# A post-norm decoder layer on one core: casts of the block sums moved from GpSimd to ScalarE, with reorders on VectorE and TensorE

## The chip, the core and the metric

The kernel runs on one NeuronCore of one Trainium2 chip. The core has five engines that run their own instruction queues side by side and meet only at semaphores: TensorE (PE: matrix products into the eight PSUM banks), VectorE (DVE), ScalarE (ACT), GpSimd (POOL) and SyncE (SP, which here only issues DMAs). An instruction that waits for a semaphore holds up everything behind it on its engine. The metric is the device time of one execution in microseconds (us), lower is better, as the median of several runs.

## What is computed

```python
x = _layernorm(x + self_attention(x))                # 8 sequences, 128 tokens, 512 features
x = _layernorm(x + cross_attention(x, ctx, mask))    # 32 heads of 128
x = _layernorm(x + feed_forward_with_experts(x))

# cross attention, where the change lies:
x = _rmsnorm(hidden_states, ln_weight)
h_q = (x @ w_q.T).reshape(b, lq, H, DH)
h_k = (key_value_states @ w_k.T).reshape(b, lk, H, DH)
h_v = (key_value_states @ w_v.T).reshape(b, lk, H, DH)
score = jnp.einsum('bqhd,bkhd->bhqk', h_q, h_k)
score = score + position_bias[None]
score = jnp.where(m, score, -jnp.inf)
score = jax.nn.softmax(score, axis=-1)
attn = jnp.einsum('bhqk,bkhd->bqhd', score, h_v).reshape(b, lq, H * DH)
out = attn @ w_out.T
```

All matrix products of weights are made in float32 from two parts: each operand is a high part (a cast to a shorter float, `_hi`) and a low part (the operand less its high part, `_lo`), and a product is hi*hi + hi*lo + lo*hi.

## The kernel before

`self_attention` is the first stage (to about 205 us), `layer` the rest. In `layer` the 32 heads go in 16 groups g of two heads, and each group is four tiles s = 0 to 3 (one head for half of the batch). Number the tiles n = 4g + s. Per tile PE makes the scores (L2060), the products ahead for a later tile, the transposes of the probabilities of tile n-1 (L2067), two v projections (L760), between them attention times v of tile n-1 (L2077, `pv`), and two output products (L2090). DVE adds mask and bias and takes the maximum (`masked_scores`, L1580 and `nmx` L1585), divides by the sum (`normalise`, L1589 to L1591), makes low parts (`at_lo` L1597, `lo` L1571, `lo_op` L1603) and adds the output to `acc` (L1634). ScalarE makes the exponentials (`exps`, L1331), the high parts and the copies out of PSUM (`prT` L1339, `v` L1324, `at_hi` L1345). POOL adds mask and bias into `bm` (`bias_mask`, L1045), which `masked_scores` needs.

Groups 0 and 1 are *plain*: the q and k projections are made directly, twelve products each (L760). Groups 2 to 15 (`SEVEN` = 2) take the projection of q and of k as a 2 x 2 block product by seven products p1 to p7 instead of eight (Strassen's scheme, L1936). `unit(w, ...)` makes one of them, w = 0 for q and w = 1 for k. That needs seven sums of x and context blocks, named S1k, S2k, S4k, S3k, S3q, S2q, S4q, and S1q, which stays in SBUF in the place of a quarter of `xnT`. POOL forms them during tiles 2 to 7: `combine` adds or subtracts 128 x 1024 numbers (L1052), `hi_of` casts (L1055), `block_lo` subtracts (L1058). SP's `keep` stores each as high and low part into `block_sums` in HBM (L970). From there POOL's `load_sums` brings one block after another into two ring slots of 1 MB (L1068) in each later group, behind a tiny *gate* instruction (L1067) that waits until the product that read the slot is over. The scratch areas are four quarters `area(0)` to `area(3)` of `stage`, and `U_` (= `mem.u`). `three_turns` (L1145 to L1153) and `last_turn` combine the weight blocks; ScalarE's `hi_op` and DVE's `lo_op` split them. `copy_p1` (L1366) copies product 1 from PSUM into the same `mem.u`.

There is no scheduler: each engine's order is written out in its block function. POOL's order in the stretch of the sums is

```python
            bias_mask(0, 2, True)
            k_differences()
            bias_mask(0, 3, True)
            k_first()
            k_fourth()
            k_second()
            bias_mask(1, 0, False)
```

and goes on with `k_fourth_split`, `k_third_split`, mask of tile 5, `q_third`, `q_second`, mask of tile 6, `q_third_split`, `q_fourth`, mask of tile 7, `q_first`, `q_second_split`, `q_fourth_split`, `q_first_split`, the first two ring loads and `three_turns(2)`.

## Time and profile before

| | us |
|---|---|
| median of 3 runs | 1101.55 (1100.03 to 1103.22) |
| the profiled execution | 1104.81 |
| its span, first to last instruction | 1103.0 |
| PE busy | 1036.4 |
| DVE busy | 764.7 |
| ScalarE busy | 501.2 |
| POOL busy | 482.1 |

The page gives for each engine its busy time; a group view gives the instructions of one line with their mean duration and the idle time of the engine ahead of them, with what ended it. A timeline gives single instructions with their start and duration. Durations on PE overlap, since products are pipelined: the distance between starts is what one costs. An idle time of an engine costs time only where that engine is the one that the end waits for.

### The profile page before, as it was taken

What the parts mean: (1) busy time and instruction counts of PE and PEld (TensorE: products, weight loads), DVE (VectorE), ACT (ScalarE), POOL (GpSimd) and SP (SyncE); (2) the same over time, 40 slices, a digit from 0 to 9 for tenths busy, and PEclk for the clock granted to TensorE, in tenths of its full rate; (3) what the DMA queues carried; (4) which work ended last, traced back from release to release, by engine and by line L of the source; (5) the groups of instructions that cost most, each with busy time, mean ns of one, the idle gap of its engine ahead of it and who ended that gap; (6) DMA issues with size and microseconds to landing.
All of it is one profiled execution on the core that took longest, in us unless ns stands there. A gap on an engine that the chain in (4) does not pass through costs nothing.

```text
span 1103.0 us, 20540 instructions
## 1 busy us (share of the span) xinstructions
PE 1036.4 (94%) x6354; PEld 898.0 (81%) x6354; DVE 764.7 (69%) x2269; ACT 501.2 (45%) x1377; POOL 482.1 (44%) x545
## 2 busy tenths in 40 slices
PE   7899989986999999999999999999999999999995
PEld 6677767876888888888888888888888888888884
DVE  5799989666667575757576666767675757576883
ACT  4889886441434343434343434444343434343421
POOL 7576665798734242423333242423242424242142
PEclk9999989998999999999999999999999999999998
DMA  4301002242355546372728374636455463636001
GB/s 149 125 18 52 2 1 68 76 157 117 131 211 184 206 141 227 120 247 100 255 95 287 95 252 140 240 139 227 155 198 192 155 212 135 247 100 232 28 20 58
DMA packets 44588, 159.77 MB, mean 145 GB/s; under 512 B 4736, under 2 KB 21504, under 8 KB 31616
## 3 DMA queue, kind: packets, MB, share of 16 engines
q0 software_dynamic: 14528, 105.91, 26.9%
q1 hardware_dynamic: 30016, 53.32, 14.8%
q8 instruction: 22, 0.36, 0.1%
q14 instruction: 22, 0.18, 0.1%
HBM read 149.78 MB, written 9.44 MB: 144 GB/s over the span
## 4 chain that ended last, share of the span: by engine, by line
PE 60%; issue 13%; DVE 11%; DMA 8%; POOL 5%; ACT 3%; POOLq 0%; SPq 0%; DVEq 0%; ACTq 0%
PE bank L1936 19%; PE bank L760 13%; PE bank L2090 12%; DMA ring<-block_sums 7%; PE bank L2077 4%; PE bank L2060 4%; PE bank L2108 3%; DVE sm L481 2%; PE bank L2067 2%; POOL bm L1045 2%; POOL pool_gate L1067 1%; POOL ring L1068 1%; DVE alpha L557 1%; DMA stage<-in_wq 1%; ACT pr L1331 1%
## 5 line engine op out<-in xcount | busy, mean ns | idle before, releaser
L1331 ACT ACTIVATE pr<-sm,nmx 128x128 f32<-128x128 f32 x256 | 99.8, 391 | 191.1 <-DVE nmx L1585 190.8
L1045 POOL TENSOR_TENSOR bm<-mask,bias 128x512 f32<-128x512 f32 x64 | 84.6, 1323 | 225.6 <-DVE nmx L1585 223.6
L1634 DVE TENSOR_TENSOR acc<-acc,bank 128x512 f32<-128x512 f32 x128 | 86.2, 684 | 81.7 <-PE bank L2090 81.7
L1067 POOL TENSOR_TENSOR pool_gate<-eps 128x1 f32<-128x1 f32 x96 | 45.5, 474 | 193.9 <-PE bank L1936 193.9
L1936 PE MATMUL bank<-ring,wqk_hi 128*128 128x512 f32 x392 | 110.9, 405 | 15.0 <-DMA ring<-block_sums 14.6
L1324 ACT COPY v<-bank 128x256 f32<-128x256 f32 x124 | 45.9, 370 | 126.8 <-PE bank L760 79.1
L2090 PE MATMUL bank<-wo_hi,at_hi 128*128 128x512 f32 x256 | 100.7, 393 | 0.3 <-DVE acc L1634 0.3
L2090 PE MATMUL bank<-wo_lo,at_hi 128*128 128x512 f32 x256 | 100.2, 391 | 0.0
L2090 PE MATMUL bank<-wo_hi,at_lo 128*128 128x512 f32 x256 | 100.0, 390 | 0.0
L1603 DVE TENSOR_TENSOR wqk_lo<-qk_raw,wqk_hi 128x512 fp32r<-128x512 f32 x98 | 92.6, 946 | 9.6 <-ACT wqk_hi L1360 9.6
L1936 PEld LDWEIGHTS bank<-ring,wqk_hi 128*128 128x128 f32 x392 | 67.8, 189 | 28.1 <-DMA ring<-block_sums 17.2
L760 PE MATMUL bank<-wv_hi,cT_hi 128*128 128x256 f32 x512 | 89.5, 297 | 0.3 <-DVE wv_lo L1891 0.3
L2077 PE MATMUL bank<-prT,v 128*128 128x128 f32 x512 | 69.9, 281 | 14.4 <-ACT prT L1339 14.4
L760 PE MATMUL bank<-wv_hi,cT_lo 128*128 128x256 f32 x512 | 82.6, 284 | 0.0
L760 PE MATMUL bank<-wv_lo,cT_hi 128*128 128x256 f32 x512 | 82.5, 284 | 0.0
L1339 ACT COPY prT<-bank 128x512 f32<-128x512 f32 x64 | 37.3, 582 | 96.2 <-PE bank L2067 96.2
L2077 PEld LDWEIGHTS bank<-prT,v 128*128 128x128 f32 x512 | 65.4, 196 | 16.9 <-ACT prT L1339 15.5
L1597 DVE TENSOR_TENSOR at_lo<-bank,at_hi 128x512 fp32r<-128x512 f32 x64 | 44.0, 687 | 48.0 <-ACT at_hi L1345 48.0
L760 PEld LDWEIGHTS bank<-wv_hi,cT_hi 128*128 128x128 f32 x512 | 73.1, 191 | 4.6 <-issue 0.5
L760 PEld LDWEIGHTS bank<-wv_hi,cT_lo 128*128 128x128 f32 x512 | 70.9, 192 | 0.0
L760 PEld LDWEIGHTS bank<-wv_lo,cT_hi 128*128 128x128 f32 x512 | 70.8, 192 | 0.0
L2060 PEld LDWEIGHTS bank<-kT,qT 128*128 128x128 f32 x512 | 66.7, 191 | 4.8
(289 smaller groups left out, 2633.0 us busy)
## 6 DMA issues: line engine op xcount, KB each, us to landing
ring<-block_sums POOLq DMA_DIRECT2D x98, 1024.0 KB, 5.6
qk_raw<-in_wqk SPq DMA_DIRECT2D x56, 256.0 KB, 5.8
o_raw<-in_wo SPq DMA_DIRECT2D x16, 512.0 KB, 3.3
v_raw<-in_wv SPq DMA_DIRECT2D x15, 512.0 KB, 8.8
block_sums<-stage SPq DMA_DIRECT2D x12, 512.0 KB, 3.6
acc<-in_x POOLq DMA_DIRECT2D x1, 2048.0 KB, 8.3
qk_raw<-in_wqk SPq DMA_DIRECT2D x4, 512.0 KB, 6.0
bias<-in_bias SPq DMA_DIRECT2D x16, 128.0 KB, 2.1
```

What stands on the lines that cost most here:

```text
L760: ins = nc.tensor.matmul(out, lhs, rhs, start=start and i == 0, stop=i == len(pairs) - 1)
L1045: nc.gpsimd.tensor_tensor(bm[:, s % 2], mask[:, HALF * (s // HG):HALF * (s // HG + 1), :], bias[:, i:i + 1, :].broadcast_to([P, HALF, T]), ...
L1067: nc.gpsimd.tensor_tensor(pool_gate[:, BLOCKS.index(name):BLOCKS.index(name) + 1], eps[:, 0:1], eps[:, 0:1], ALU.add)
L1324: nc.scalar.copy(v[:, b, :], PX[b % 2][:, 0:HG * DH2]).then_inc(s_vc, 1)
L1331: e = nc.scalar.activation(pr[:, s % 2, k], sm[:, s % 2, k], ACT.Exp, bias=nmx[:, s % 2, k:k + 1], accum_out=sums[:, s % 2, k:k + 1])
L1597: nc.vector.tensor_tensor(at[1][:, s // HG, i], PO[:], f32(at[0][:, s // HG, i]), ALU.subtract).then_inc(s_al, 1)
L1603: nc.vector.tensor_tensor(part_of(slot, 1), block_of(qk_raw, raw), f32(part_of(slot, 0)), ALU.subtract).then_inc(s_op, 1)
L1634: nc.vector.tensor_tensor(acc[:, b], acc[:, b], PX[b % 2][:], ALU.add).then_inc(s_acc, 1)
L1936: ins = nc.tensor.matmul((PQ, PK)[w][:], lhs, rhs, start=i == 0, stop=i == len(pairs) - 1)
L2060: ins = nc.tensor.matmul(S[s % 2][:, tok], qT[:, s % 2, tok], kT[:, s % 2, tok], start=True, stop=True)
L2077: ins = nc.tensor.matmul(PO[:, k * T:(k + 1) * T], v[:, half * HALF + k, i * DH2:(i + 1) * DH2], prT[:, k], start=True, stop=True)
L2090: ins = nc.tensor.matmul(PX[b % 2][:], at[p][:, half, i, tok], wo[q][:, i, :], start=k == 0 and (p, q) == PARTS[0], stop=k == HG - 1 and ( ...
```

## The change

- `combine` and `block_lo` on POOL work in two halves of 512 columns each, where they took 1024 in one instruction.
- The eight casts (`hi_of`) leave POOL. ScalarE makes them in `sums_hi`, at the ends of tiles: S1k at the end of tile 2, S2k and S4k of tile 3, S3k of tile 4, S3q of tile 5, S2q, S4q and S1q of tile 6. It waits there for POOL's sums (`s_made`, counted in halves) and, where it overwrites an area, until the block in it is stored. `block_lo` waits for the cast (`s_sums_h`). The semaphore `s_s1q` goes; `s_ready` counts its step too.
- DVE makes the masked scores ahead of `lo(wo, ...)` in the plain tiles with s = 2.
- DVE's `experts_constants` (13 small instructions) moves from the end of tile 3 to tile 60, in the last group.
- In the seven-product groups product 5 is made for k (w = 1) ahead of q (w = 0), and DVE adds them in that order.
- In `hi_op` the wait for the products of A11 is on q's counter instead of k's.

```diff
-                sp.wait_ge(s_ready, BLOCKS.index(name) + 1)
+                sp.wait_ge(s_ready, 2 * BLOCKS.index(name) + 2)
...
             def combine(out, in0, in1, op):
-                made.link(nc.gpsimd.tensor_tensor(out, in0, in1, op))
-
-            def hi_of(out, raw):
-                made.link(nc.gpsimd.tensor_copy(out, raw))
+                for c in range(2):
+                    made.link(nc.gpsimd.tensor_tensor(out[:, c], in0[:, c], in1[:, c], op))
 
             def block_lo(name, out, raw, hi):
-                nc.gpsimd.tensor_tensor(out, raw, f32(hi), ALU.subtract).then_inc(s_ready, 1)
-                pool.wait_ge(s_ready, BLOCKS.index(name) + 1)
+                pool.wait_ge(s_sums_h, BLOCKS.index(name) + 1)
+                for c in range(2):
+                    nc.gpsimd.tensor_tensor(out[:, c], raw[:, c], f32(hi[:, c]), ALU.subtract).then_inc(s_ready, 1)
+                    pool.wait_ge(s_ready, 2 * BLOCKS.index(name) + c + 1)
...
             def k_second():
-                wait_kept(pool, "S1k")
-                hi_of(area(0, F32R), area(3))
                 block_lo("S2k", area(3, F32R), area(3), area(0, F32R))
...
             def q_first_split():
-                pool.wait_ge(s_q, TILES * SEVEN)
-                hi_of(quarter(xnT[0], 0, 1), area(2))
+                pool.wait_ge(s_sums_h, len(BLOCKS) + 1)
                 nc.gpsimd.tensor_tensor(quarter(xnT[1], 0, 1), area(2), f32(quarter(xnT[0], 0, 1)), ALU.subtract)\
-                    .then_inc(s_s1q, 1)
+                    .then_inc(s_ready, 1)
...
-                        act.wait_ge(s_unit[1], done(UNITS, g - 1, {"A11": "p5", "A22": "p3", "A12": "p7", "T2": "p4"}[name]))
+                        w, unit = {"A11": (0, "p5"), "A22": (1, "p3"), "A12": (1, "p7"), "T2": (1, "p4")}[name]
+                        act.wait_ge(s_unit[w], done(UNITS, g - 1, unit))
...
+            def sums_hi(name, out, raw, made, kept):
+                act.wait_ge(s_made, made)
+                if kept is not None:
+                    wait_kept(act, kept)
+                if name == "S1q":
+                    act.wait_ge(s_q, TILES * SEVEN)
+                nc.scalar.copy(out, raw).then_inc(s_sums_h, 1)
...
+                if first and s == 2:
+                    sums_hi("S1k", area(0, F32R), mem.u[:], 10, None)
+                if first and s == 3:
+                    sums_hi("S2k", area(0, F32R), area(3), 6, "S1k")
+                    sums_hi("S4k", area(1, F32R), mem.u[:], 14, "S1k")
+                if seven_next and s == 0:
+                    sums_hi("S3k", area(0, F32R), area(2), 6, "S2k")
+                if seven_next and s == 1:
+                    sums_hi("S3q", area(0, F32R), area(3), 20, "S3k")
+                if s == 2 and seven_next:
+                    sums_hi("S2q", area(0, F32R), mem.u[:], 24, "S3q")
+                    sums_hi("S4q", area(3, F32R), area(1), 28, "S3q")
+                    sums_hi("S1q", quarter(xnT[0], 0, 1), area(2), 32, None)
                 if s == 2 and seven_next:
                     hi_op(g + 1, "A12")
                     copy_p1(g + 1, 0)
...
+                masked_scores(n, s, first, link)
                 if s == 2:
                     lo(wo, o_raw, s_wo_h, s_wo, g + 1)
-                masked_scores(n, s, first, link)
                 if first and s == 0:
...
-                if first and s == TILES - 1:
-                    experts_constants()
 
...
+                    sum_w(g, 1)
+                    lo_op(g, "T3")
                     sum_w(g, 0)
-                    lo_op(g, "T3")
-                    sum_w(g, 1)
                     normalise(n, s, link)
                     lo_op(g, "T4")
                     at_lo(n - 1, sp, head)
                     sum_c21(g, 0)
                     sum_c21(g, 1)
+                    if last:
+                        experts_constants()
...
-                    pe.wait_ge(s_s1q, 1)
+                    pe.wait_ge(s_ready, 2 * len(BLOCKS) + 1)
...
+                    product_5(g, 1)
                     product_5(g, 0)
-                    product_5(g, 1)
```

How this moves instructions, in the program's own order (names are output <- inputs, a count behind where one repeats).

POOL at the start of the sums, from the mask of tile 3 to the mask of tile 4. `stage` holds the areas, `u` is `U_`. Before:

```order
L1045 TENSOR_TENSOR bm<-mask,bias 128x512
L1052 TENSOR_TENSOR u<-stage,cT_hi 128x1024
L1052 TENSOR_TENSOR u<-u,cT_lo 128x1024
L1055 CAST stage<-u 128x1024
L1058 TENSOR_TENSOR stage<-u,stage 128x1024
L1052 TENSOR_TENSOR u<-cT_hi,stage 128x1024
L1052 TENSOR_TENSOR u<-u,cT_lo 128x1024
L1055 CAST stage<-stage 128x1024
L1058 TENSOR_TENSOR stage<-stage 128x1024
L1045 TENSOR_TENSOR bm<-mask,bias 128x512
```

and after:

```order
L1046 TENSOR_TENSOR bm<-mask,bias 128x512
L1054 TENSOR_TENSOR u<-stage,cT_hi 128x512 x2
L1054 TENSOR_TENSOR u<-u,cT_lo 128x512 x2
L1059 TENSOR_TENSOR stage<-u,stage 128x512 x2
L1054 TENSOR_TENSOR u<-cT_hi,stage 128x512 x2
L1054 TENSOR_TENSOR u<-u,cT_lo 128x512 x2
L1059 TENSOR_TENSOR stage<-stage 128x512 x2
L1046 TENSOR_TENSOR bm<-mask,bias 128x512
```

The casts are gone, and what was one instruction of 1024 columns is two of 512; the order of the rest is kept.

ScalarE at the end of tile 6 and the start of tile 7. Before:

```order
L1324 COPY v<-bank 128x256
L1345 CAST at_hi<-bank 128x512
L1324 COPY v<-bank 128x256
L1360 CAST wqk_hi<-qk_raw 128x2x256
L1366 COPY u<-bank 128x512 x2
L1331 ACTIVATE pr,sums<-sm,nmx 128x128 x4
```

and after:

```order
L1313 COPY v<-bank 128x256
L1334 CAST at_hi<-bank 128x512
L1313 COPY v<-bank 128x256
L1358 CAST stage<-u 128x1024
L1358 CAST stage<-stage 128x1024
L1358 CAST xnT_hi<-stage 128x2x512
L1350 CAST wqk_hi<-qk_raw 128x2x256
L1364 COPY u<-bank 128x512 x2
L1320 ACTIVATE pr,sums<-sm,nmx 128x128 x4
```

The casts of S2q, S4q and S1q stand ahead of the high part of the weights A12, the two copies of product 1 and the exponentials of tile 7.

PE at the start of a group in the loop, product 5: bank2 is q's and bank0 is k's, `ring0` the slot that S1k comes into. Before:

```order
L2060 MATMUL bank4<-kT,qT 128x128 x4
L1960 REGISTER_ALU
L1965 REGISTER_ALU
L1936 MATMUL bank2<-xnT_hi,wqk0_hi 128x512 x2
L1936 MATMUL bank2<-xnT_lo,wqk0_hi 128x512 x2
L1936 MATMUL bank2<-xnT_hi,wqk0_lo 128x512 x2
L1964 ISA
L1936 MATMUL bank0<-ring0_49,wqk0_hi 128x512 x4
L1936 MATMUL bank0<-ring0_49,wqk0_lo 128x512 x2
```

and after:

```order
L2071 MATMUL bank4<-kT,qT 128x128 x4
L1971 REGISTER_ALU
L1975 ISA
L1976 REGISTER_ALU
L1947 MATMUL bank0<-ring0_49,wqk0_hi 128x512 x4
L1947 MATMUL bank0<-ring0_49,wqk0_lo 128x512 x2
L1947 MATMUL bank2<-xnT_hi,wqk0_hi 128x512 x2
L1947 MATMUL bank2<-xnT_lo,wqk0_hi 128x512 x2
L1947 MATMUL bank2<-xnT_hi,wqk0_lo 128x512 x2
```

The product that reads the ring now stands right behind the scores.

## Rows read from the trace of the kernel before

**Rows 1.** The page's first part: an engine's busy us, share of the span, instructions

```profile
PE 1036.4 (94%) x6354; PEld 898.0 (81%) x6354; DVE 764.7 (69%) x2269; ACT 501.2 (45%) x1377; POOL 482.1 (44%) x545
```

**Rows 2.** Groups by line: busy us, mean ns | idle before, releaser

```profile
L1936 PE MATMUL bank<-ring,wqk_hi 128*128 128x512 f32 x392 | 110.9, 405 | 15.0 <-DMA ring<-block_sums 14.6 <-issue 0.4
...
L2077 PE MATMUL bank<-prT,v 128*128 128x128 f32 x512 | 69.9, 281 | 14.4 <-ACT prT L1339 14.4
```

**Rows 3.** Timeline of PE, tiles 2 to 6: start us, duration, [idle before]

```profile
230.88 2.08 PE L2077 MATMUL bank<-prT,v 128*128 128x128 f32 x8 [3.23 <-ACT prT L1339]
...
269.52 2.08 PE L2077 MATMUL bank<-prT,v 128*128 128x128 f32 x8 [8.62 <-ACT prT L1339]
...
277.20 1.05 PE L2060 MATMUL bank<-kT,qT 128*128 128x128 f32 x8
...
290.58 1.05 PE L2060 MATMUL bank<-kT,qT 128*128 128x128 f32 x8
```

**Rows 4.** Windows: us, busy by engine (x), then clock, DMA share, GB/s

```profile
231.00:235.00 4.00, 4.00 (x22) 3.96 (x23) 2.40 (x2) 0.93 (x3) 3.87 (x2) 0.63 0.50 204
...
269.50:277.00 7.50, 7.48 (x32) 6.89 (x33) 3.60 (x3) 1.23 (x3) 6.77 (x3) 0.64 0.35 140
```

**Rows 5.** Timeline of DVE, tiles 2 to 4

```profile
222.10 3.33 DVE L1571 TENSOR_TENSOR wo_lo<-o_raw,wo_hi 128x1024 fp32r<-128x1024 f32 x1
...
226.32 1.39 DVE L1585 TENSOR_SCALAR nmx<-mx 128x4 f32<-128x4 f32 x1
...
254.46 2.46 DVE L1700 TENSOR_SCALAR count<-iota_in,active_f 128x16 f32<-128x16 f32 x1
...
264.97 0.18 DVE L1706 TENSOR_TENSOR logit<-logit,hit 128x16 f32<-128x16 f32 x1
```

**Rows 6.** Timeline of POOL, tiles 2 to 6: sums, a cast, a mask, ring loads

```profile
220.96 3.38 POOL L1052 TENSOR_TENSOR u<-stage,cT_hi 128x1024 f32<-128x1024 f32 x1
...
237.50 1.04 POOL L1055 CAST stage<-stage 128x1024 fp32r<-128x1024 f32 x1
...
250.77 1.29 POOL L1045 TENSOR_TENSOR bm<-mask,bias 128x512 f32<-128x512 f32 x1
...
256.96 2.39 POOL L1052 TENSOR_TENSOR stage<-stage 128x1024 f32<-128x1024 f32 x1
...
299.41 1.15 POOL L1068 DMA_DIRECT2D ring<-block_sums  x2 [0.59 <-POOL xnT_lo L1139]
```

**Rows 7.** Timeline of ScalarE: a cast of 1024 columns

```profile
288.31 1.05 ACT L1304 CAST wv_hi<-v_raw 128x1024 fp32r<-128x1024 f32 x1
```

**Rows 8.** DMA issues of 225 to 300 us: count, KB, median us to landing

```profile
block_sums<-stage SPq DMA_DIRECT2D x12, 512.0 KB, 3.6
...
block_sums<-u SPq DMA_DIRECT2D x2, 512.0 KB, 4.7
```

**Rows 9.** Chain that ended last, products 2 and 6: start us, us, what

```profile
308.69 2.78 PE bank L1936 x12
...
314.23 1.42 PE bank L1936 x6
```

**Rows 10.** Timeline of PE, one group of the loop: products 5 and 3

```profile
426.45 0.71 PE L1936 MATMUL bank<-xnT_hi,wqk_hi 128*128 128x512 f32 x2
...
436.26 1.20 PE L1936 MATMUL bank<-ring,wqk_hi 128*128 128x512 f32 x4 [1.16 <-DMA ring<-block_sums]
```

**Rows 11.** Timeline of POOL, same group: the mask and S4k's load

```profile
428.12 1.29 POOL L1045 TENSOR_TENSOR bm<-mask,bias 128x512 f32<-128x512 f32 x1 [4.24 <-DVE nmx L1585]
...
429.96 0.58 POOL L1068 DMA_DIRECT2D ring<-block_sums  x1
```

**Rows 12.** Same group, the `ring` tile's issues of 420 to 422 us: S1k's load

```profile
L1068 POOL DMA_DIRECT2D ring<-block_sums x1: 580/580/580, 420.8 to 420.8; - x1
DMA to landing us min/median/max: 6.4/6.4/6.4
```

**Rows 13.** Timeline of DVE, tile 61

```profile
1021.17 0.69 DVE L1597 TENSOR_TENSOR at_lo<-bank,at_hi 128x512 fp32r<-128x512 f32 x1 [1.03 <-ACT at_hi L1345]
```

More of the change, by code:

```diff
@@ L902, in layer @@
         s_ring = [sem("b_sums_in_even"), sem("b_sums_in_odd")]
-        s_made, s_s1q = sem("b_sums_made"), sem("b_sums_q1")
+        s_sums_h = sem("b_sums_hi")
+        s_made = sem("b_sums_made")
         s_ready = sem("b_sums_ready")
@@ L1082, in k_first @@
                 combine(U_, U_, f32(quarter(cT[1], 0, 0)), ALU.add)
-                hi_of(area(0, F32R), U_)
                 block_lo("S1k", area(1, F32R), U_, area(0, F32R))
@@ L1090, in k_second @@
             def k_second():
-                wait_kept(pool, "S1k")
-                hi_of(area(0, F32R), area(3))
                 block_lo("S2k", area(3, F32R), area(3), area(0, F32R))
             def k_fourth_split():
-                hi_of(area(1, F32R), U_)
                 block_lo("S4k", U_.bitcast(F32R), U_, area(1, F32R))
             def k_third_split():
-                wait_kept(pool, "S2k")
-                hi_of(area(0, F32R), area(2))
                 block_lo("S3k", area(2, F32R), area(2), area(0, F32R))
@@ L1114, in q_third_split @@
             def q_third_split():
-                wait_kept(pool, "S3k")
-                hi_of(area(0, F32R), area(3))
                 block_lo("S3q", area(3, F32R), area(3), area(0, F32R))
@@ L1127, in q_second_split @@
             def q_second_split():
-                wait_kept(pool, "S3q")
-                hi_of(area(0, F32R), U_)
                 block_lo("S2q", U_.bitcast(F32R), U_, area(0, F32R))
             def q_fourth_split():
-                hi_of(area(3, F32R), area(1))
                 block_lo("S4q", area(1, F32R), area(1), area(3, F32R))
             def q_first_split():
-                pool.wait_ge(s_q, TILES * SEVEN)
-                hi_of(quarter(xnT[0], 0, 1), area(2))
+                pool.wait_ge(s_sums_h, len(BLOCKS) + 1)
                 nc.gpsimd.tensor_tensor(quarter(xnT[1], 0, 1), area(2), f32(quarter(xnT[0], 0, 1)), ALU.subtract)\
-                    .then_inc(s_s1q, 1)
+                    .then_inc(s_ready, 1)
             def three_turns(g):
@@ L1248, in _ @@
                 wait_kept(pool, name)
-            pool.wait_ge(s_s1q, 1)
+            pool.wait_ge(s_ready, 2 * len(BLOCKS) + 1)
             load_sums(SEVEN, "S2q")
```

## The prediction

> **What bounds the kernel now.** I read the page's first part, then the groups of instructions with what ended the idle time before them, then the timelines of the two stretches where TensorE idles. TensorE (PE) is busy for 1036.4 us, 94% of the span [rows 1], so a gain can only be PE's idle time, or its slow clock after an idle. Two groups carry what this diff touches [rows 2]: 14.4 us of idle before L2077 (attention times v) for ScalarE's `prT`, all in the plain tiles, and 14.6 us before L1936 for a `ring` load from `block_sums`, in 13 pieces, one in each seven-product group but the last.
>
> Number a tile n = 4g + s. Tiles 2 to 7 are the stretch of 219 to 308 us in which GpSimd (POOL) forms the block sums. A tile without a stall takes 13.38 us (the scores of tiles 5 and 6 start at 277.20 and 290.58) [rows 3]. PE waits 3.23 us in tile 2 and 8.62 us in tile 4 [rows 3], and restarts slowly: at 0.63 of the clock for 4.0 us and at 0.64 for 7.5 us [rows 4], so 4.0 x 0.37 = 1.5 and 7.5 x 0.36 = 2.7 us more. Both waits begin on VectorE (DVE). In tile 2 `wo_lo` stands ahead of the masked scores and takes 3.33 us; then the 4-element `nmx` takes 1.39. In tile 4 the chain of `experts_constants` runs from the end of tile 3 to 265.15; a 16-element op of it takes 2.46 us, though others take 0.18 [rows 5]. What stretches them is POOL: each ends as a POOL instruction of about 2.4 us ends (3.38 where POOL itself had to wait) [rows 6]. DVE instructions with both inputs in SBUF exclude POOL's, one whole instruction at a time.
>
> **Part by part, tiles 2 to 7.** (1) Masked scores ahead of `wo_lo` at s = 2: they can start at about 223 instead of 225.4 and `nmx` waits for half a POOL instruction, so the exponentials of tile 2 start near 224.2 instead of 227.7. The 3.23 and its 1.5 of clock go; next late is `at_lo` of tile 1 at about 231.2, just when PE wants it: 0.1. (2) Without the constants tile 4's 8.62 + 2.7 go. Their cost where they land, tile 60: 13 small ops at 0.18 + 0.03 = 2.7 us on DVE, ahead of two `acc` additions and the masked scores. By tile 61 about 0.3 of it is left, and there DVE stood idle for 1.03 us before `at_lo`, waiting for ScalarE [rows 13]. So zero; without that cover about 1. (3) Tile 3 keeps some 0.6 of stall, ScalarE's two table loads. Tile 5 would then start at 277.2 - (3.2 + 1.5 + 0.6 + 8.6 + 2.7) = 260.6.
>
> (4) POOL is what comes next. The eight casts it loses take 1.04 us each when nothing interferes [rows 6]. Sixteen sums and seven low parts are split: a POOL op of 512 columns takes 1.29, one of 1024 takes 2.39 [rows 6], so two halves with a gap of 0.08 each take 2.74 against 2.47, and 23 of them add 6.2 us; the casts with their gaps save 9. [...]
>
> But each low part now waits for ScalarE, and ScalarE casts only at the end of a tile. The sums for S2k's part are ready early, its cast is not: it stands behind tile 3's last v copy, at 244.5 to 245.6, and POOL, done with the fourth sum at about 241, idles 4.6. S3k's cast stands behind tile 4's last v copy: tile 5's start less the 2.7 of output products, 257.9 to 258.95 with the 1.05 that ScalarE takes for 1024 columns [rows 7]. POOL finished S4k's low part at 252.4 and idles 6.6. S1k costs 1.5. Against that the 5.4 us go in which POOL waited for the late `nmx` of before.
>
> From 259.0 POOL has 22 halves and three masks before the last sum (S1q) is made: 25 x 1.37 = 34.3, so 293.3. DVE's conflicting ops in this time (`wv_lo`, `wo_lo`, two normalisations, A11, A22) are worth 4.5 us; where POOL is not ready anyway they cost nothing. I take 3.2, so 296.5; the ends are 2 and 5, so 295.3 and 298.3. Behind that moment T a row of ScalarE work is queued that was free before, because the cast of S1q waits for T in order ahead of `hi_op` A12, both copies of product 1, and tile 7's exponentials. Copy 0 also overwrites U, so it waits until S2q's low part (T + 2.7) is stored: with 0.35 for the first issue and 4.7 from issue to landing [rows 8] it runs at T + 7.8. PE has product 1 behind it at about 294 and stands until T + 8.4 = 304.9, against product 2 at 308.69 before [rows 9]. At half clock again (2.7) its way to product 6 is 2.8 + 0.4 + 1.4 + 0.9 more: T + 16.6. POOL's way is as long: S4q and S1q low to T + 8.0, S4q's store (3.6 [rows 8], with issue) to T + 9.8, two ring loads 1.15 [rows 6], three turns of 1.38, then the T2 cast 0.6 and its low part 0.7: T + 16.6 also. Product 6 so starts at 313.1, and 314.23 before [rows 9]: 1.1 gained. Then the next S1k load stands behind two masks and a turn on POOL that used to be over: 0.6 back. **Tiles 2 to 7 and the hand-over: 0.5 us faster**, with -3 and +3 as ends. Some 17 us of PE idle vanish and are given back before product 2 and product 6.
>
> **The 13 groups.** Product 3 for k waits 1.16 us for S4k [rows 10]. That load goes out at 429.96, behind a mask that ends at 428.12 + 1.29 = 429.41 and a gate that waited for product 5 for k [rows 11]. With k first, product 5 can't start at 426.45 [rows 10]: its own S1k lands at 420.8 + 6.4 = 427.2 [rows 12]. So 0.75 us of new wait, all products after it 0.75 later, and k done at about 429.0, before the mask is. The mask then sets the load: 429.5 to 429.8 by the length of the gate, 0.15 to 0.45 earlier. If it lands as much earlier, at about 436.05, PE arrives at 435.85 and waits 0.2. Gain per group: 0.15 to 0.35; if the transfer itself is what is slow, 0. I take 0.2 x 13 = **2.6**, ends 0 and 4.6. Of the swap in DVE's sums nothing is seen: product 3 for q comes 5 us later.
>
> **The sum.** 0.5 + 2.6 = 3.1. The profiled execution took 1104.81 (span 1103.0), so 1101.7 for it; on the median of 1101.55, which is 3.3 below it, 1098.4.
>
> **Rivals.** (a) *POOL is earlier than I think.* For it: the lock costs POOL little where it idles, and halves let DVE in sooner. T = 293.3, the sum without any conflict, gives product 6 at 309.9, 4.3 gained, less 0.6; with 2.6 of the groups 6.3: **1095.2**. Against it: six conflicting ops stand in this stretch.
> (b) *Slower: ScalarE's casts close the circle.* ScalarE, queued behind a cast, delays the exponentials; they delay PE's tile end; that delays the next cast; POOL idles longer. The place is S3q's cast (needs the sum at about 272, ScalarE is there at 271.4) and S4q's and S1q's in tile 6. It decides when T passes 298.3, 1.1 + 0.7 later than taken. With one tile end missed by POOL's two halves more and a mask (4.1), T = 300.6 and product 6 is at 317.2, 3.0 late, and 0.6 more; with nothing gained in the groups: **1105.1**, with 2.6 gained 1102.5.
> (c) *The wait of product 3 only moves to product 5.* The engines of the transfers are loaded from the S1k issue to product 3; then an earlier issue lands no earlier. Groups 0, tiles 0.5: **1101.0**.
> (d) *The exclusion is smaller than an instruction.* The Trainium skill (SBUF — State Buffer, "Who interferes with whom") says that a DVE instruction with two SBUF inputs contends with a GpSimd instruction that reads SBUF, and that the loser blocks for the whole instruction. By that rule halves shorten each block and gain nothing in sum; the trace agrees (1.39 us for 4 elements [rows 5]). As a mechanism from the rows: if DVE, asking oftener, wins between all halves, `nmx` and the rest are short but POOL pays each conflict in full, 4.5 and not 3.2: T + 1.3, 1.3 less gained: 1099.7, within the forecast's own range.
>
> **How the numbers follow.** A measurement of this kernel can tell about 0.3% (3.3 us) from no change. Forecast 0.48 (1095.8 to 1101.5; its middle is close to the 0.3% bound, I put 0.20 of it beyond), (a) 0.23, (b) 0.14, (c) with (d) 0.15. Faster by over 0.3%: 0.20 + 0.22 = 0.42. Slower by over 0.3%: 0.09 of (b) and 0.03 for what is not seen, 0.12. Same: 0.46. The range takes in (a) and most of (b): 1093.0 to 1104.0.
>
> **What would show it.** Right: no `prT` wait over 1 us in tiles 2 to 4; tile 5's scores near 260.6; POOL idle of 4 to 7 us before the low parts of S2k and S3k; a PE wait of some 10 us before product 2 of group 2, for ScalarE's copy, and slow clock behind it; product 6 near 313; in each later group a ring wait of 0.7 before product 5 for k and one of 0.2 before product 3 for k. Wrong: product 6 before 311 (POOL's conflicts mis-sized), or a PE wait before product 3 for k that is still 1.1 with 0.7 before product 5 (the groups would be slower), or a stall in tile 61.

## The result and the profile after

| | before | after |
|---|---|---|
| median of 13 runs each, us | 1102.22 (1100.03 to 1104.03) | 1099.15 (1097.21 to 1101.35) |
| profiled execution, us | 1104.81 | 1099.65 |
| its span, us | 1103.0 | 1097.7 |

The ratio is 0.9974 with a 95% interval of 0.9965 to 0.9982: 2.9 us less, under the 0.3% that a measurement here can tell, and 0.75 us from the forecast of 1098.4. The sum was right and two of its terms were not. The tiles up to the hand-over became 3.3 us slower where 0.5 faster was predicted, and the seven-product groups became 6.0 us faster where 2.6 was predicted. The two errors, 3.8 and 3.4 us, cancel: that the total came out so close is luck.

The groups of instructions by line of the changed kernel (busy us, mean ns | idle before, releaser), which answer to [rows 2]:

```profile
L1947 PE MATMUL bank<-ring,wqk_hi 128*128 128x512 f32 x392 | 111.4, 406 | 11.8 <-DMA ring<-block_sums 8.6 <-DVE wqk_lo L1614 2.8 <-issue 0.3
...
L2088 PE MATMUL bank<-prT,v 128*128 128x128 f32 x512 | 68.3, 276 | 3.0 <-ACT prT L1328 3.0
...
L1947 PE MATMUL bank<-xnT_hi,wqk_hi 128*128 128x512 f32 x112 | 39.2, 431 | 9.0 <-ACT u L1364 9.0
```

The wait for `prT` went from 14.4 us to 3.0 and the wait for the ring from 14.6 to 8.6, but 9.0 us for ScalarE's copy of product 1 and 2.8 us for a low part are new. The timeline of PE (start, duration, [idle before]), which answers to [rows 3] and [rows 9], shows where:

```profile
257.91 1.05 PE L2071 MATMUL bank<-kT,qT 128*128 128x128 f32 x8
...
281.68 1.56 PE L2088 MATMUL bank<-prT,v 128*128 128x128 f32 x8 [1.91 <-ACT prT L1328]
...
301.25 1.19 PE L1947 MATMUL bank<-xnT_hi,wqk_hi 128*128 128x512 f32 x2 [9.01 <-ACT u L1364]
...
312.07 1.32 PE L1947 MATMUL bank<-ring,wqk_hi 128*128 128x512 f32 x4 [2.77 <-DVE wqk_lo L1614]
...
320.69 1.05 PE L2071 MATMUL bank<-kT,qT 128*128 128x128 f32 x8
324.25 1.18 PE L1947 MATMUL bank<-ring,wqk_hi 128*128 128x512 f32 x4 [2.51 <-DMA ring<-block_sums]
```

The execution shown reached tile 2 at 216.79 us and that of before at 219.18; the first stage, which the change doesn't touch, differs by such amounts between executions. So 2.39 is added to compare. Tile 5's scores are then at 260.30 (predicted 260.6), product 2 at 303.64, product 6 at 314.46 and the scores of group 2 at 323.08. The idles of 3.23 and 8.62 us are gone, and some 12 us stand before product 2 and product 6 in their place. The 1.91 us in tile 6 cost nothing by themselves, since PE then stands for 9.01 us in any case.

GpSimd (POOL) in the same stretch, as [rows 6], then VectorE's (DVE) `nmx` of tile 2, as [rows 5]:

```profile
229.09 2.65 POOL L1059 TENSOR_TENSOR stage<-u,stage 128x512 fp32r<-128x512 f32 x2 [1.60 <-ACT stage L1358]
...
243.45 2.66 POOL L1059 TENSOR_TENSOR stage<-stage 128x512 fp32r<-128x512 f32 x2 [4.99 <-ACT stage L1358]
...
256.83 2.65 POOL L1059 TENSOR_TENSOR stage<-stage 128x512 fp32r<-128x512 f32 x2 [6.74 <-ACT stage L1358]
...
291.26 2.61 POOL L1054 TENSOR_TENSOR stage<-stage,xnT_lo 128x512 f32<-128x512 f32 x2
...
304.69 1.15 POOL L1069 DMA_DIRECT2D ring<-block_sums  x2 [2.69 <-DMA block_sums<-stage]
```

```profile
221.34 0.30 DVE L1596 TENSOR_SCALAR nmx<-mx 128x4 f32<-128x4 f32 x1
```

POOL idles for the casts 1.60, 4.99 and 6.74 us, against 1.5, 4.6 and 6.6 predicted. The last sum is made at 293.87 (291.26 + 2.61), which is 296.26 of before's time; T was predicted as 296.5. The same moment of before is 285.70, where this row of its POOL ends, so POOL is now 10.6 us later.

```profile
283.30 2.40 POOL L1052 TENSOR_TENSOR stage<-stage,xnT_lo 128x1024 f32<-128x1024 f32 x1
```

What follows the sum is in these rows of ScalarE, the cast of S1q and the two copies of product 1, and in the windows after three restarts of PE (columns as in [rows 4]):

```profile
293.90 1.04 ACT L1358 CAST xnT_hi<-stage 128x1024 fp32r<-128x1024 f32 x1 [5.62 <-POOL stage L1054]
300.52 1.07 ACT L1364 COPY u<-bank 128x512 f32<-128x512 f32 x2 [5.05 <-DMA block_sums<-u]
```

```profile
281.70:285.60 3.90, 3.90 (x21) 3.90 (x21) 3.90 (x3) 1.83 (x4) 3.66 (x4) 0.57 0.64 255
...
301.25:305.00 3.75, 3.75 (x9) 3.01 (x10) 0.69 (x1) 1.88 (x9) 1.06 (x2) 0.50 0.94 321
...
312.10:316.00 3.90, 3.90 (x16) 3.48 (x17) 2.30 (x3) 0.07 (x1) 3.42 (x4) 0.62 0.27 84
```

PE runs at 0.50 of its clock after the 9.01 us, at its lower level of 1.2 GHz. After the 1.91 us the mean of the window is 0.57 and after the 2.77 it is 0.62, so part of each window is at the lower level.

A later group, the one of [rows 10] and [rows 11]: PE, then POOL with the gate, then where S4k's load lands.

```profile
425.97 1.05 PE L2071 MATMUL bank<-kT,qT 128*128 128x128 f32 x8
427.63 1.18 PE L1947 MATMUL bank<-ring,wqk_hi 128*128 128x512 f32 x4 [0.61 <-DMA ring<-block_sums]
```

```profile
428.45 1.29 POOL L1046 TENSOR_TENSOR bm<-mask,bias 128x512 f32<-128x512 f32 x1 [4.25 <-DVE nmx L1596]
429.71 0.18 POOL L1068 TENSOR_TENSOR pool_gate<-eps 128x1 f32<-128x1 f32 x1
429.84 0.58 POOL L1069 DMA_DIRECT2D ring<-block_sums  x1
```

```profile
L1069 POOL DMA_DIRECT2D ring<-block_sums x1: 577/577/577, 429.8 to 429.8; - x1
...
DMA to landing us min/median/max: 5.2/5.2/5.2
```

Product 5 waits 0.61 for k and product 3 waits for nothing here. Between the scores of group 3 and those of tile 60 lie 620.36 us (374.26 to 994.62); before it was 626.32 (373.40 to 999.72). That is 5.96 less in 12 groups, 0.50 each.

The groups are not all alike. Before, T3's low part stood on VectorE 0.84 us ahead of the gate, and the gate took 0.43 in each of the 12 groups. In the changed kernel it takes 0.18 in seven groups, in which T3 starts behind it, and 0.64 to 0.72 in five, in which T3 starts ahead of it by as little as 0.01 us. The gate and T3 in one of the five:

```profile
481.38 0.72 POOL L1068 TENSOR_TENSOR pool_gate<-eps 128x1 f32<-128x1 f32 x1
```

```profile
481.36 0.68 DVE L1614 TENSOR_TENSOR wqk_lo<-qk_raw,wqk_hi 128x512 fp32r<-128x512 f32 x1
```

In the seven groups S4k's load goes out 3.87 us after the scores and lands in 5.1 to 5.5 us; in the five it goes out at 4.3 to 4.4, as it did before (4.32), and takes 5.6 to 6.1.

### The profile page after: what moved, and what is told of

Its sections match the earlier page's. It is cut to its first block, busy times and chain, and to the rows that moved or that the text cites. A ratio compares the mean times of both kernels' runs of the same rounds, so it can differ in the third digit from the quotient of the medians.

```text
span 1097.7 us, 20558 instructions
## 1 busy us (share of the span) xinstructions
PE 1034.4 (94%) x6354; PEld 894.8 (82%) x6354; DVE 744.4 (68%) x2269; ACT 508.4 (46%) x1385; POOL 478.4 (44%) x560
## 3 DMA queue, kind: packets, MB, share of 16 engines
q1 hardware_dynamic: 30016, 53.32, 14.6%
## 4 chain that ended last, share of the span: by engine, by line
PE 66%; DMA 9%; POOL 8%; DVE 7%; issue 6%; ACT 3%; SPq 0%; POOLq 0%; DVEq 0%; ACTq 0%
PE bank L1947 22%; PE bank L760 16%; PE bank L2101 12%; DMA ring<-block_sums 8%; PE bank L2088 5%; PE bank L2071 4%; PE bank L2119 3%; PE bank L2078 2%; POOL stage L1054 2%; DVE sm L481 2%; ACT pr L410 1%; POOL sm L322 1%; POOL stage L1059 1%; POOL pool_gate L1068 1%; POOL bm L1046 1%
## 5 line engine op out<-in xcount | busy, mean ns | idle before, releaser
L1947 PE MATMUL bank<-ring,wqk_hi 128*128 128x512 f32 x392 | 111.4, 406 | 11.8 <-DMA ring<-block_sums 8.6
L1614 DVE TENSOR_TENSOR wqk_lo<-qk_raw,wqk_hi 128x512 fp32r<-128x512 f32 x98 | 89.0, 909 | 19.2 <-ACT wqk_hi L1350 19.2
```

The source lines that it names most:

```text
L1614: nc.vector.tensor_tensor(part_of(slot, 1), block_of(qk_raw, raw), f32(part_of(slot, 0)), ALU.subtract).then_inc(s_op, 1)
L1947: ins = nc.tensor.matmul((PQ, PK)[w][:], lhs, rhs, start=i == 0, stop=i == len(pairs) - 1)
```

## The experiments

**Theory A**: the whole gain is the swap in the groups, and all that is done on POOL and ScalarE up to the hand-over costs more than the two reorders there bring. **Theory B**: the parts are as predicted, about even up to the hand-over and 2.6 us from the swap. A third theory asks for each wait whether it was removed or only moved. The differences below are (1 - ratio) x 1102. The interval of each ratio is 1 to 2 us to either side, so a difference between two changed kernels is known to about 2 us.

### The swap alone, and all but the swap

The kernel before with product 5's halves swapped (and the waits that go with it):

```diff
                 elif s == 0:
-                    product_5(g, 0)
                     product_5(g, 1)
+                    product_5(g, 0)
```

> The kernel before with the swap of product 5 alone (PE's order, VectorE's order of the two sums, the wait in hi_op); casts, whole POOL instructions and the other orders as before. Theory A, from the trace of the changed kernel: a group took 51.7 us there and 52.24 before, so the swap is worth 0.5 to 0.6 in each of 12 or 13 groups: 6 to 7.5 us less than before, about 1095; group period 51.7; S4k's load lands some 5.2 us after its issue and product 3 for k does not wait. Rival B, my own prediction: 0.2 a group, 2.6 less, about 1099.6. Rival C: the period fell for another reason of the change, and the swap alone only moves the wait: within 1 us of before.

Measured: 1096.89 us, ratio 0.9941 (0.9929 to 0.9954), 6.5 us less.

The changed kernel with those lines put back:

> The changed kernel with the swap of product 5 undone. Theory A: the rest of the change loses 3 to 4 us between tile 2 and the scores of group 3, so with no swap the kernel is slower than before: about 1105 (before + 3.3). Rival B: the rest is worth 0.5, so about 1101.7, no different from before. The group period goes back to 52.24 by both.

Measured: 1106.3 us, ratio 1.0032 (1.0021 to 1.0044), 3.5 us more. A row of PE from it, product 3 for k in the same group, and POOL's load of S4k in the kernel with the swap alone:

```profile
436.40 1.20 PE L1946 MATMUL bank<-ring,wqk_hi 128*128 128x512 f32 x4 [1.26 <-DMA ring<-block_sums]
```

```profile
427.18 0.58 POOL L1068 DMA_DIRECT2D ring<-block_sums  x1
```

Theory A holds. The swap is worth 6.5 us alone and 6.4 in the changed kernel (1.0032 against 0.9974), and the rest of the change costs 3.5. Without the swap the wait of 1.2 us before product 3 is back.

### The casts back on GpSimd, and the reorders alone

The changed kernel, with the eight casts on POOL again and the halves kept:

```diff
             def block_lo(name, out, raw, hi):
-                pool.wait_ge(s_sums_h, BLOCKS.index(name) + 1)
...
             def k_second():
+                wait_kept(pool, "S1k")
+                hi_of(area(0, F32R), area(3))
                 block_lo("S2k", area(3, F32R), area(3), area(0, F32R))
```

> The changed kernel with the eight casts back on POOL, at the places where they were; half instructions, swap and reorders stay. Theory A: POOL's idle of 1.6 + 5.0 + 6.7 us for ScalarE's casts costs more than the eight casts of about 9 us, and the copy of product 1 is no longer queued behind the cast of S1q: product 6 starts 4 to 6 us earlier than in the changed kernel and the time is about 1094 (1092 to 1096). Rival B: the casts on POOL block VectorE and make POOL later by as much as the idle gives: 1099, as changed. Rival C: POOL later by the whole 9: 1103 or more.

Measured: 1094.49 us, ratio 0.992 (0.9907 to 0.9934), 8.8 us less than before and 5.9 less than the changed kernel. PE's rows:

```profile
294.99 1.19 PE L1948 MATMUL bank<-xnT_hi,wqk_hi 128*128 128x512 f32 x2 [6.47 <-ACT u L1378]
...
306.55 2.08 PE L1948 MATMUL bank<-ring,wqk_hi 128*128 128x512 f32 x4 [4.19 <-DVE wqk_lo L1615]
```

The kernel before with only the masked scores ahead of `wo_lo` and the constants in the last group; sums unsplit, casts on POOL, no swap:

> The kernel before with two of the reorders alone: masked scores ahead of wo_lo at s = 2 of the plain tiles, and the constants of the experts in the last group. No halves, no casts on ScalarE, no swap. Theory A: the 3.2 + 8.6 us of idle and most of the slow clock go, PE comes to product 2 some 10 us or more earlier and then waits for POOL, whose chain is only shorter by the 5.4 us in which it waited for a late nmx: product 6 starts 6 to 9 us earlier than before and the kernel takes 1094 to 1096. Rival B: whole instructions of 2.4 us on POOL keep VectorE late (the halves were needed): 2 to 3 us less than before, 1099.5. Rival C: nothing is gained, since product 6 waits for POOL's ring loads as before: 1102.

Measured: 1097.53 us, ratio 0.9952 (0.9939 to 0.9966), 5.3 us less. All of PE's stalls of over 1 us between tile 2 and group 2:

```profile
230.73 0.61 PE L2090 MATMUL bank<-wo_hi,at_lo 128*128 128x512 f32 x1 [2.09 <-DVE at_lo L1597]
...
244.56 2.04 PE L2077 MATMUL bank<-prT,v 128*128 128x128 f32 x8 [2.02 <-ACT prT L1339]
...
292.56 0.80 PE L2090 MATMUL bank<-wo_hi,at_lo 128*128 128x512 f32 x1 [2.55 <-DVE at_lo L1597]
```

No wait is left before product 2 or product 6: PE is late there and not POOL. The last sum on POOL tells the parts apart; its row, in the kernel with the reorders alone and then in the one with the casts back on POOL:

```profile
275.76 2.41 POOL L1052 TENSOR_TENSOR stage<-stage,xnT_lo 128x1024 f32<-128x1024 f32 x1
```

```profile
283.52 2.99 POOL L1054 TENSOR_TENSOR stage<-stage,xnT_lo 128x512 f32<-128x512 f32 x2
```

Tile 2 starts at 216.52 and 216.06 in these. In before's time the sum is made at 285.7 before, 280.8 with the reorders alone, 289.6 with halves and POOL's own casts, 296.3 in the changed kernel. So the reorders brought POOL 4.9 us forward, the halves took 8.8 and the casts on ScalarE 6.7.

### The reorders and the swap together

> The kernel before with three reorders of the change (masked scores ahead of the wo split in tiles 2 and 6, the experts' constants at the end, product 5's two halves swapped with the order of the sums on VectorE), without the halves on GpSimd and without the casts on ScalarE. Alone the swap gave -6.1 us, the other two reorders -5.5. Theory A (they work in different stretches and add): 1102.2 - 6.1 - 5.5 = 1090.6 us, and what the changed kernel loses against it, some 8.5 us, is the price of the halves and the casts. Theory B (the earlier tiles run into the same last load before the hand-over, so that only one of the two is had there): 1094 to 1097 us.

Measured: 1088.95 us, ratio 0.9887 (0.9872 to 0.9902), 12.5 us less. PE, the two restarts after tile 6:

```profile
304.12 1.20 PE L1937 MATMUL bank<-ring,wqk_hi 128*128 128x512 f32 x4 [1.53 <-DVE wqk_lo L1604]
...
313.40 1.20 PE L1937 MATMUL bank<-ring,wqk_hi 128*128 128x512 f32 x4 [1.16 <-DMA ring<-block_sums]
```

5.3 and 6.5 make 11.8: they add, and theory B of this run (only one of the two is had) falls. The change's parts are now priced one by one, the last two each to about 2 us:

| part | us | from |
|---|---|---|
| two reorders on VectorE | -5.3 | alone |
| swap of product 5's halves | -6.5 | alone |
| halves on GpSimd | +3.6 | 0.9887 to 0.992 |
| eight casts on ScalarE | +5.9 | 0.992 to 0.9974 |

Their sum is -2.3, and the changed kernel measured -2.9. How the loss divides between halves and casts is the loosest part: from tile 2 to the end, the one profiled execution of each kernel gives 7.8 us for the halves and 4.4 for the casts. That both cost time is shown by either reckoning.

### Two of the casts earlier on ScalarE

```diff
                     copy_prT(n - 1, False)
+                if first and s == 3:
+                    sums_hi("S2k", area(0, F32R), area(3), 6, "S1k")
+                if seven_next and s == 0:
+                    sums_hi("S3k", area(0, F32R), area(2), 6, "S2k")
...
                 if first and s == 3:
-                    sums_hi("S2k", area(0, F32R), area(3), 6, "S1k")
                     sums_hi("S4k", area(1, F32R), mem.u[:], 14, "S1k")
-                if seven_next and s == 0:
-                    sums_hi("S3k", area(0, F32R), area(2), 6, "S2k")
```

> The changed kernel with two of ScalarE's eight high-part casts (S2k and S3k) moved up in their tile, ahead of the copies of v. Theory A (GpSimd is the chain before the hand-over, and its idle time of 5.0 and 6.7 us in front of those two casts comes from their late place on ScalarE): the two waits shrink by 2 to 3 us each, the last sum S1q is made 4 to 6 us earlier than at 296.3, product 2 waits correspondingly less, and the time is 3 to 5 us below the changed kernel's: 1094 to 1096 us. Theory B (ScalarE itself is needed where the casts now stand): the copies of v come a microsecond later and TensorE waits for them twice, and the time taken out before the hand-over is given back there: 1097 to 1100 us.

Measured: 1095.24 us, ratio 0.9939 (0.9925 to 0.9953), 3.9 us less than the changed kernel. POOL:

```profile
240.82 2.68 POOL L1059 TENSOR_TENSOR stage<-stage 128x512 fp32r<-128x512 f32 x2 [1.90 <-ACT stage L1358]
...
253.77 2.66 POOL L1059 TENSOR_TENSOR stage<-stage 128x512 fp32r<-128x512 f32 x2 [6.29 <-ACT stage L1358]
...
301.65 1.15 POOL L1069 DMA_DIRECT2D ring<-block_sums  x2 [2.78 <-DMA block_sums<-stage]
```

The first idle fell by 3.1 us, the second by 0.5 only, since POOL now comes to it earlier. The two ring loads go out 84.4 us after tile 2 starts, against 87.9, and 3.9 us of time follow from 3.5 us of POOL. So in the changed kernel GpSimd, waiting for casts that ScalarE makes at a fixed place, is the chain up to the hand-over.

### VectorE's order behind the swap

```diff
                 if s == 0:
-                    sum_w(g, 1)
                     lo_op(g, "T3")
+                    sum_w(g, 1)
                     sum_w(g, 0)
```

> The changed kernel with one line moved on VectorE: in each seven-product group the low part T3 stands ahead of both sums of product 1 again, not between them, so SyncE sends the weight load d about 1.5 us earlier, close behind the load of S4k (before the change the two stood 0.2 us apart, after it about 1.0 us). Theory A (S4k lands in 5.2 us in place of 6.3 because the load d, which runs on the same 16 DMA engines, starts later): the landing goes back towards 6.3 us, product 5's wait for k grows from 0.6 to about 1.1 to 1.5, and the 13 groups give back some 0.5 each, 6 us at most: 1101 to 1105 us. Theory B (the quicker landing has another cause): landing stays at 5.2 to 5.5 and the wait at 0.6, time 1098 to 1100 us. In both, the sums of product 1 are written some 1.5 us later, which costs nothing unless a wait of TensorE on VectorE's sum turns up in the products.

Measured: 1102.42 us, ratio 1.0016 (1.0003 to 1.0029), 4.6 us more than the changed kernel, in the range of theory A. POOL's mask and S4k's load, and the landing, then VectorE:

```profile
428.98 1.69 POOL L1046 TENSOR_TENSOR bm<-mask,bias 128x512 f32<-128x512 f32 x1 [4.25 <-DVE nmx L1596]
...
430.77 0.58 POOL L1069 DMA_DIRECT2D ring<-block_sums  x1
```

```profile
L1069 POOL DMA_DIRECT2D ring<-block_sums x1: 580/580/580, 430.8 to 430.8; - x1
...
DMA to landing us min/median/max: 5.4/5.4/5.4
```

```profile
428.82 0.69 DVE L1614 TENSOR_TENSOR wqk_lo<-qk_raw,wqk_hi 128x512 fp32r<-128x512 f32 x1
```

Two things moved. The weight load now goes out 1.05 us ahead of S4k in every group, and S4k lands in 5.4 us in this group but in 5.2 to 6.3 over the 12, where the seven groups of the changed kernel with the short gate took 5.1 to 5.5: that is theory A's effect, in about half of the groups. And T3's low part starts on VectorE 0.16 us ahead of the mask, so that the mask takes 1.69 us in every group and not 1.29. Counted from the group's scores (426.50), S4k is issued at 4.27 and not 3.87 (429.84 - 425.97). The waits for the ring are 18 in the trace against 15, and 9.4 us against 8.6. How the 4.6 us divide isn't shown: in the profiled execution the 12 groups take 621.88 us, only 1.5 more than the 620.36 of the changed kernel.

### The transposes ahead of product 5

```diff
+                    if not plain and s == 0:
+                        transposes(n - 1, sp)
                     products_ahead(g, s, first, last, plain, plain_next)
-                    transposes(n - 1, sp)
+                    if plain or s != 0:
+                        transposes(n - 1, sp)
```

> The changed kernel, and in each seven-product group TensorE does the transposes of the tile before ahead of product 5 and not behind it. Theory A: product 5's wait for k (0.61 us in the middle groups, for the sums' load) is real time of TensorE, and the transposes (0.4 to 0.5 us of matmuls that need no load) fill it: 0.4 to 0.5 less in each of 13 groups, so 5 to 6 us faster than the changed kernel, 1093 to 1094 us; the wait that is left is 0.1 to 0.2. Theory B: the transposes need the previous tile's softmax from VectorE and would wait themselves, or ScalarE's copies behind them come at another time and hold a later step: the wait only changes its name, 1098 to 1100 us.

Measured: 1096.39 us, ratio 0.9946 (0.9929 to 0.9963), 3.1 us less than the changed kernel. PE in two groups, product 5, then product 3:

```profile
426.80 1.19 PE L1947 MATMUL bank<-ring,wqk_hi 128*128 128x512 f32 x4 [0.21 <-DMA ring<-block_sums]
...
486.86 1.20 PE L1947 MATMUL bank<-ring,wqk_hi 128*128 128x512 f32 x4 [0.90 <-DMA ring<-block_sums]
```

Between the theories: the wait at product 5 fell by 0.4 as hoped, but product 3 waits 0.6 to 0.95 in five of the groups, and all waits for the ring went from 8.6 us to 6.1. In those groups S4k is what comes last. They are exactly the five in which T3 starts ahead of the gate (by 0.02 to 0.06 us): the gate takes 0.67 to 0.72, and S4k goes out at 4.35 to 4.39 and lands in 5.8 to 6.1. In the other seven it goes out at 3.86 to 3.88 and lands in 5.1 to 5.3, and product 3 doesn't wait.

### The best version

> The kernel with the reorders and the swap (12 us faster than the kernel before) and in each seven-product group TensorE's transposes of the tile before ahead of product 5. With the transposes moved in the changed kernel, product 5's wait fell from 0.6 to 0.2 us but product 3 waited 0.6 to 0.9 us for S4k, and 3 us of the 5 to 6 hoped for came. Theory A (the ring's loads bound the group, and TensorE's order only decides at which product the rest of the wait shows): the same 3 us again and no more, 1085 to 1087 us. Theory B (the place without the halves differs, nothing is gained): 1088 to 1090 us.

Measured: 1085.33 us, ratio 0.9853 (0.9837 to 0.9869). The transposes bring 3.7 us on this base. In the profiled execution (1082.82, the fastest of the four) T3 is ahead of the gate in one of the 12 groups only, and the waits for the ring are 1.0 us in all against 7.3 without the transposes. Theory A, that the rest of the wait must show at another product, doesn't hold for that execution.

```diff
-                if s == 2 and seven_next:
-                    lo_op(g + 1, "A11")
-                    lo_op(g + 1, "A22")
                 if not (first and s == 0):
                     at_lo(n - 1, sp, heads_of(first or s == 0)[sp])
+                if s == 2 and seven_next:
+                    lo_op(g + 1, "A11")
+                    lo_op(g + 1, "A22")
```

> The kernel with the reorders and the swap, and on VectorE in tiles 2 and 6 the low part of the attention output (at_lo) ahead of the splits that stand before it and are not needed in that tile (the wqk split of 3.41 us in tile 2, the low parts A11 and A22 of 4.33 us together in tile 6). These take that long, in place of 1.2 and 1.4, since GpSimd works on the same stretch. Theory A: the two waits of TensorE for at_lo (2.09 and 1.79 us) go; what is late next is A22 for product 6 (it waits 1.5 us already), so 2 to 4 us are gained of 3.9: 1085 to 1087 us. Theory B (VectorE only does the same blocked work later, and product 6 and the first loads after the hand-over take the whole gain): 1088 to 1090 us.

Measured: 1087.37 us, ratio 0.9867 (0.9851 to 0.9883), 2.2 us less than without it by the ratios, whose intervals overlap. The waits for `at_lo` are gone, but in PE's timeline product 6 stands longer (1.53 without the edit):

```profile
302.11 1.19 PE L1939 MATMUL bank<-ring,wqk_hi 128*128 128x512 f32 x4 [2.95 <-DVE wqk_lo L1604]
```

> Both of the other two edits together, transposes ahead of product 5 in the groups and at_lo first in tiles 2 and 6. They stand in different stretches, so by the theory that each stretch is bound by itself they add: 12.0 + 3 + 3 = 18 us below the kernel before, 1082 to 1085 us. If the hand-over takes back what is gained ahead of it, this is no faster than the kernel with the transposes alone, 1085 to 1087 us.

Measured: 1084.95 us, ratio 0.9839 (0.9825 to 0.9854). That is 17.7 us less than the kernel before and the fastest here, but against the 0.9853 of the transposes alone it is no difference that these runs can tell. The second edit isn't shown to be worth anything on top of the first.

## Why the prediction was right, and where it was not

**Removing the two stalls: right.** No `prT` wait over 1 us is left in tiles 2 to 4, `nmx` takes 0.30, and tile 5 starts 0.3 from the predicted place. Steps (1), (2) and (3) of the part by part hold. The reorders alone bring 5.3 us, though there stalls of 2.09, 2.02 and 2.55 us are left in tiles 2, 3 and 6, the middle one for `prT`.

**The constants at the end: free, as said.** In tile 61 VectorE's row of [rows 13] still shows a gap before `at_lo` in the changed kernel:

```profile
1015.92 0.69 DVE L1608 TENSOR_TENSOR at_lo<-bank,at_hi 128x512 fp32r<-128x512 f32 x1 [1.04 <-ACT at_hi L1334]
```

It was 1.03. From tile 60's scores to tile 61's are 13.52 us (13.60 before), and from there to tile 62's 8.34 (8.42 before).

**POOL up to T: right.** All three idles were right within 0.4 us, and T within 0.3. With it the reading that some 17 us vanish and are given back later held.

**From T to group 2: the step that failed.** Product 2 came at T + 7.4 where T + 8.4 was said. Product 6 came at T + 18.2 and not T + 16.6. The two ring loads waited for S4q's store until T + 10.8 (9.8 was said); from there three turns and the low part T2 (1.09 us, not 0.7) were 0.6 longer. So product 6 came 0.23 late and not 1.1 early by [rows 9]; by PE's timeline, where it started at 313.99 before, 0.47 late. Then a term was missing altogether. After its 2.77 us of idle PE restarts at 0.62 of the clock for 3.9 us, and from product 6 to group 2's scores take 8.62 us where 7.05 were needed before: 1.57 lost. The prediction had PE and POOL reach product 6 at the same moment, T + 16.6, so it had no wait there and no slow clock behind one. PE was ready at T + 15.4, POOL's way was 1.6 us longer than said, and the 2.77 us between them brought the slow clock. Last, S1k's first load is issued at 314.94, and the rows of SyncE's queue have weight loads of 256, 256 and 512 KB around it:

```profile
313.89 1.07 SPq L965 DMA_DIRECT2D qk_raw<-in_wqk  x2
315.15 0.35 SPq L936 DMA_DIRECT2D v_raw<-in_wv  x1
```

Two of them leave ahead of S1k, and it lands in 9.2 us. Before, S1k left at 316.18 and the first of them at 316.36, and it landed in 5.6. The other runs agree: it landed in 5.5 to 5.7 in the three others in which it left 0.2 ahead of them, and in 9.1 to 9.2 in the four others in which it left 1.04 to 1.05 behind the first; at 0.55 and 1.33 behind it took 6.6 to 8.4. So in before's time it is there 4.7 us later (326.5 against 321.8), and the swap has product 5 ask for it first. Product 5 waits 2.51, of which 1.2 is lost by group 3 (period 53.57 against 52.36), and 0.6 was said. In sum 0.47 + 1.57 + 1.21 = 3.25 slower. Of this the 1.21 needs the swap, by which k is asked for first: without it group 2 takes 52.41 us, as before. The kernel without the swap is 2.1 us slower in its trace up to group 2's scores and 0.6 in the 12 groups, against 3.5 (2.3 to 4.8) by the ratio.

**The groups: mechanism right, size wrong.** The wait at product 5 was put at 0.75 and is 0.61, and 0.20 to 0.64 over the 12 groups. The 0.2 left at product 3 is zero in ten of them. In seven groups the issue of S4k moved by 0.45 relative to the scores (4.32 to 3.87), the end of the range given; in five it hardly moved. The prediction left the difference to "the length of the gate" and said that of the swap in DVE's sums nothing is seen; the gate's length is decided by whether VectorE's T3, which stands behind the first of these sums, starts ahead of it. And the term "if it lands as much earlier" was mis-sized: the transfer took 5.2 us and not 6.3. Before, S4k and the weight load left 0.2 us apart (429.96 and 430.16) and took 6.3 and 5.8; afterwards the weight load leaves 1.0 later and they take 5.2 and 5.0. Over the 12 groups S4k took 6.0 to 6.6 before, and in tile 60, where no weight load leaves near it, 5.1. So 0.50 x 12 and not 0.2 x 13.

**The rivals.** (c), that the wait only moves and nothing is gained, is false for the swap, where 1.16 us at product 3 became 0.61 at product 5, and partly true for the transposes, where product 3 took back nearly half of what was expected. (b), the circle through ScalarE, named the right cause, ScalarE's casts, and they cost 5.9 us, but not in the way that it said. The circle did not close: the casts make T 6.7 us later, which the forecast of T had in it, and what the forecast missed stands behind T. (d) has a part in it: 16 sums and five low parts are split ahead of T, and at 0.27 each they would cost 5.7 us, and the halves moved T by 8.8. POOL's halved pairs beside VectorE's work last up to 4.6 us where most unsplit instructions stand at 2.4. Added up to T, POOL's instructions take 9.1 us more than their undisturbed lengths with the halves (casts on POOL) and 5.8 without, and these 3.3 us are the rest. The Trainium skill (SBUF — State Buffer, "Who interferes with whom") says that the loser of the port blocks for the other's whole instruction. By that rule shorter instructions shorten each block and give VectorE more turns, and the 3.3 us agree; that each of them is such a block was not shown. Nor are `nmx` and the 16-element op of [rows 5] cases of the two-input rule that (d) names: both are TENSOR_SCALARs with one input tensor, and they show only that each ends as POOL's instruction does.

## What to carry to other kernels

Price each part of a compound change by itself: here two reorders and one swap were worth 12 us, and what was done on POOL and ScalarE, the halves and the casts that the change is named for, cost nearly 10 of it. Work moved to an idle engine is done only where that engine's program order puts it; what counts is how long the giver then stands waiting, and what is next in line behind its last result. Where a forecast has two engines arrive at the same moment, an error of a microsecond in either is a stall, and it needs a term for the slow clock behind it: stalls of 1.91 and 2.77 us had one here. And look at all rounds of a loop before reading a number from one: here seven of 12 groups went one way and five the other.

## What the runs showed of the hardware

- A transfer's time depends on what leaves beside it within a microsecond. In the groups the same 1 MB landed in 5.1 us with no weight load near it (tile 60), in 5.1 to 5.5 where one of 0.25 MB left 0.8 to 1.0 later, in 5.6 to 6.6 where it left 0.2 later, and in 5.2 to 6.3 where it left 1.05 earlier (before, the changed kernel, T3 first). At the hand-over it landed in 5.5 to 5.7 us where it left 0.2 ahead of 1 MB of weight loads, and in 9.1 to 9.2 where part of these had left 1.05 ahead of it.
- Which of two engines starts first by a few hundredths of a microsecond decides who waits. The gate on GpSimd, 128 x 1, takes 0.18 us when VectorE's subtraction T3 starts behind it and 0.64 to 0.72 when it starts 0.01 to 0.18 us ahead, in 7 and 5 of the 12 groups; in the five, S4k then leaves only 0.2 us ahead of the weight load, in the seven 0.8 to 1.0.
- A VectorE subtraction that starts 0.16 us ahead of a GpSimd mask stretches it from 1.29 to 1.69 us, in all 12 groups.
- Two halves of 512 columns took 2.60 to 2.66 us on GpSimd undisturbed, and one instruction of 1024 took 2.39.
- How long a stall of PE is doesn't tell alone whether a slow clock follows: the windows of 3.3 to 3.9 us behind stalls of 1.79 and 2.16 us are at 1.00 (reorders and swap), that behind 1.91 us at 0.57 (changed kernel).
